# First attention of a four-layer kernel: the multiply by the inverse input scale moves from VectorE to ScalarE

## What is computed

```python
def _div_clamp_fp8(x, scale):
    y = jnp.clip(x.astype(jnp.float32) / scale, -FP8_MAX, FP8_MAX)
    y = y.astype(jnp.bfloat16).astype(jnp.float32)
    return _fp8_roundtrip(y)

def _fp8_linear_pertensor(x, wq, w_scale, in_scale):
    xq = _div_clamp_fp8(x, in_scale)
    return jnp.einsum('bsi,oi->bso', xq * in_scale, wq) * w_scale

ln_out = _ln(hidden_states, ln_w, ln_b)
q = _ln(_fp8_linear_pertensor(ln_out, wq, wq_scale, q_in_scale).reshape(...), qln_w, qln_b)
k = ...; v = ...
core = _gqa(q, k, v)
qx = ...; kx, vx = the context's projections
xout = _gqa(qx, kx, vx)
catq = _div_clamp_fp8(jnp.concatenate([core, xout], axis=-1), proj_smooth)
return jnp.einsum('bsi,oi->bso', catq, wproj) * (proj_in_scale * proj_w_scale)
```

## Time and profile before

| | |
|---|---|
| median of 3 runs | 1549.01 us (1548.94 to 1551.25) |
| the profiled execution | 1549.62 us, span 1547.8 us |
| mean granted TensorE clock | 0.982 |
| busy, share of the span | TensorE matmul 94%, VectorE 59%, ScalarE 48%, GpSimd 34% |
| first attention | from the start to about 474 us |

### The profile page before, as it was taken

How to read it: one execution, slowest core, us unless ns; L and a number is a source line. 1 busy time by engine, 2 the same in 40 slices (tenths; PEclk the granted TensorE clock), 3 DMA queues, 4 the chain that set the end, 5 groups by cost and what they waited for, 6 DMA issues and landing times. The chain is left out here.

```text
span 1547.8 us, 22216 instructions
## 1 busy us (share of the span) xinstructions
PE 1450.4 (94%) x6910; PEld 1040.0 (67%) x6910; DVE 911.0 (59%) x1972; ACT 749.6 (48%) x2052; POOL 527.3 (34%) x519
## 2 busy tenths in 40 slices
PE   3999999899989999999999999999968999989998
PEld 1677777777774565557787979777745666665656
DVE  7899988899975342323465454554677555553322
ACT  3888788888872211110343535343456555544210
POOL 2667577877761000000542424222111333321000
PEclk9999999999999999999999999999979999999999
DMA  4201000200006411112100000002041000001110
GB/s 197 89 32 61 5 5 1 94 1 1 1 1 271 162 54 51 52 50 75 65 1 1 1 1 1 28 0 78 28 194 45 0 1 1 1 28 35 51 63 22
DMA packets 21304, 71.66 MB, mean 46 GB/s; under 512 B 3858, under 2 KB 6290, under 8 KB 18244
## 3 DMA queue, kind: packets, MB, share of 16 engines
q1 hardware_dynamic: 12980, 57.37, 9.9%
q10 hardware_dynamic: 8208, 12.87, 2.6%
HBM read 69.01 MB, written 1.22 MB: 45 GB/s over the span
## 5 line engine op out<-in xcount | busy, mean ns | idle before, releaser
L1170 ACT ACTIVATE l0f_silu<-bank 128x512 f32<-128x512 f32 x48 | 28.6, 597 | 199.4 <-PE bank L1094 183.1
L808 POOL TENSOR_TENSOR l0a_stepped<-l0a_y,l0a_m 128x512 f32<-128x512 bf16 x64 | 74.1, 1158 | 99.6 <-DVE l0a_m L573 99.1
L1273 DVE TENSOR_TENSOR l0f_product<-l0f_silu,bank 128x512 f32<-128x512 f32 x48 | 32.9, 687 | 124.7 <-ACT l0f_silu L1170 124.5
L836 POOL TENSOR_TENSOR l0a_head_rstd<-l0a_head_var,all_minus_half 128x4 f32<-128x4 f32 x96 | 99.2, 1038 | 6.9 <-DVE l0a_head_var L602 6.9
L749 ACT ACTIVATE l0a_work<-bank,l0a_neg_max 128x128 f32<-128x128 f32 x256 | 90.5, 368 | 5.3 <-DVE l0a_neg_max L615 5.1
L1710 DVE TENSOR_TENSOR all_weights_a<-bank,all_cols 128x512 f32<-128x512 f32 x64 | 43.9, 690 | 79.3 <-PE bank L1539 47.3
L1106 PEld LDWEIGHTS bank<-all_weights_a,l0f_hidden 128*128 128x128 f32 x384 | 72.9, 190 | 25.2 <-issue 16.7
L1106 PE MATMUL bank<-all_weights_a,l0f_hidden 128*128 128x256 f32 x384 | 88.9, 379 | 0.0
L425 PEld LDWEIGHTS bank<-l0a_k_t,l0a_q_t 128*128 128x128 f32 x512 | 64.3, 191 | 33.8 <-ACT l0a_q_t L735 27.4
L2588 POOL TENSOR_TENSOR l3a_q_scale<-l3a_q_var,all_minus_half 128x4 f32<-128x4 f32 x32 | 32.4, 1013 | 159.7 <-DVE l3a_q_var L2378 159.7
L2298 PE MATMUL bank<-l3a_f_xn_t,all_weights_b 128*128 128x512 f32 x192 | 86.2, 593 | 0.0
(11 more groups left out here) (434 smaller groups left out, 3801.0 us busy)
## 6 DMA issues: line engine op xcount, KB each, us to landing
l0f_spread<-l0f_weights ACTq DMA_DIRECT2D x32, 192.0 KB, 2.7
all_weights_a<-in_l_w_q SPq DMA_DIRECT2D x2, 2048.0 KB, 14.2
l0f_spread<-l0f_weights ACTq DMA_DIRECT2D x32, 128.0 KB, 2.9
all_weights_b<-in_l_e_gate_up SPq DMA_DIRECT2D x1, 3200.0 KB, 10.2
all_weights_b<-in_l_e_gate SPq DMA_DIRECT2D x1, 3072.0 KB, 10.7
all_weights_a<-in_l_e_up SPq DMA_DIRECT2D x4, 768.0 KB, 6.9
all_weights_a<-in_l_e_down SPq DMA_DIRECT2D x1, 3072.0 KB, 15.4
l3a_spread<-l3f_weights SPq DMA_DIRECT2D x10, 256.0 KB, 3.5
```

The costliest lines, as they stand in the source:

```text
L808: done = g.tensor_tensor(stepped[:, 0:n], value, step, ALU.add)
L836: g.tensor_tensor(head_rstd[:, m % 2, :], head_var[:, m % 2, :], res.minus_half[:, 0:HU], ALU.pow)\
```

## The change

The multiply leaves VectorE. ScalarE does it in two activations (one for each chunk of 128 features, since the scale is one column for each), of 128 x 128 elements each, from `ln_t` to `yq16`. `scale_input` is last in ScalarE's list, due in steps 1, 3 and 7, so behind the squares of those steps; the early parts are scaled in steps 5, 7, 23 and 31 of tile 3. The waits for GpSimd's end with `yq16` (`quant_done`, `early_done`) move along to ScalarE, and VectorE waits for a new semaphore of ScalarE instead. The first tile's part is scaled ahead of ScalarE's first weight work.

```diff
+        quant_scaled = Steady(mem, "l0a_quant_scaled", 3)
+        early_scaled = mem.sem("l0a_early_scaled")
-        EARLY_TILE, EARLY_QUANT = 3, [6, 8, 24, 32]
+        EARLY_TILE, EARLY_SCALE, EARLY_QUANT = 3, [5, 7, 23, 31], [6, 8, 24, 32]
@@ VectorE
-            def quantise_part(b, i):
-                core, t = divmod(b, TILES)
+            def quantise_part(i):
                 part = slice(i * D, (i + 1) * D)
-                v.tensor_tensor(yq16[:, part].rearrange("p (c n) -> p c n", c=KC), ln_t[:, :, t * P:(t + 1) * P],
-                                along(inv_in[:, KC * (core + i):KC * (core + i + 1)], P), ALU.mult)
                 return split(yq16[:, part], mq16[:, part], D)
...
-                v.wait_ge(ln_ready, TILES)
-                quant_done.wait(v, quant_done.at(b - 1, i + 1))
-                if b == TILES + 2 and i > 0:
-                    v.wait_ge(early_done, len(EARLY))
-                quantise_part(b, i).then_inc(quant_split.sem, 3 // quant_parts(b))
+                quant_scaled.wait(v, quant_scaled.at(b, i + 1))
+                quantise_part(i).then_inc(quant_split.sem, 3 // quant_parts(b))
 
             def quantise_early(k):
-                if k > 1:
-                    v.wait_ge(early_done, k - 1)
-                quantise_part(*EARLY[k]).then_inc(early_split, 1)
+                v.wait_ge(early_scaled, k + 1)
+                quantise_part(EARLY[k][1]).then_inc(early_split, 1)
@@ ScalarE
+            def scale_part(b, i):
+                core, t = divmod(b, TILES)
+                for c in range(KC):
+                    at = KC * (core + i) + c
+                    done = act.activation(yq16[:, (KC * i + c) * P:(KC * i + c + 1) * P], ln_t[:, c, t * P:(t + 1) * P],
+                                          ACT.Copy, scale=inv_in[:, at:at + 1])
+                return done
+
+            def scale_input(b, i):
+
+                b += 1
+                if b == VTS or i >= quant_parts(b):
+                    return
+                quant_done.wait(act, quant_done.at(b - 1, i + 1))
+                if b == TILES + 2 and i > 0:
+                    act.wait_ge(early_done, len(EARLY))
+                scale_part(b, i).then_inc(quant_scaled.sem, 3 // quant_parts(b))
+
+            def scale_early(k):
+                if k > 1:
+                    act.wait_ge(early_done, k - 1)
+                scale_part(*EARLY[k]).then_inc(early_scaled, 1)
...
+            scale_input(-1, 0)
             high(0)
...
+                               (scale_input, [1, 3, 7]), in_tile(EARLY_TILE, scale_early, EARLY_SCALE),
```

## The result

The changed kernel takes 1542.6 us (median of 7 runs, 1540.0 to 1545.1) against 1548.8 for the kernel before (7 runs). The ratio is 0.9961 with a 95% interval of 0.9951 to 0.9970: faster by 6.2 us, between 4.6 and 7.6. Forecast was 1543.2, with a range of 1535 to 1548.

What follows compares the result with a forecast made beforehand. VectorE was taken to set the pace, partly standing behind GpSimd's tensor operations. The terms -4.5 - 1.0 - 0.9 + 0.6 gave -5.8 us, so 1543.2 us, with a range of 1535 to 1548.

Steps and rivals of the forecast that it cites:

- What bounds the kernel: First attention: VectorE sets the pace, but its two-SBUF-input and short bf16 operations stand until GpSimd's tensor operation is over.
- Third parts: Nine parts, six tiles' third and the last three early ones: removing the multiply saves 0.5 us each, 4.5 us.
- First and second parts: 19 ordinary parts of both passes from the third tile on: GpSimd's chain leaves 0.05 us saved each, 1.0 us.
- the two behind weight operations: Two multiplies behind a GpSimd subtraction held up by a weight operation: about 0.45 us saved each, 0.9 us.
- ScalarE's work after the first tile: Added scaling, 0.6 us a part, hidden by ScalarE's idle time before squares: cost taken as 0, bounds 0 to 3 us.
- a margin of 1.29: Second pass, step 4: exponentials end 1.29 us before VectorE wants them; 0.9 us of lateness leaves 0.4.
- 1.1 us of TensorE's idle time a tile: Second pass: idle time before turns takes up a query turned 0.6 to 0.9 us late.
- its 0.4 us a tile: Price if the exponentials' cover goes: VectorE waits 0.4 us a tile at worst, at 0.8 us a part.
- Rival C: ScalarE and TensorE become the bound through exponentials and turned query: about 7 us slower, 1556 us; chance 0.08.
- a sign of C: TensorE waiting above 1 us a tile for the turned query, and VectorE waiting for L749, would show ScalarE and TensorE bounding.
- The first tile's 0.6 us: First tile: VectorE waits for ScalarE there, so one part of added scaling is paid, 0.6 us.
- The total: Whole kernel: 5.8 us less, 1543.2 us as the median of the runs; this forecast's chance 0.60.

Runs made afterwards that it cites:

- e7: Kernel before, with GpSimd's add and subtraction of the mixed heads on 4 columns instead of 512 after the first two uses; 1523.1 us, ratio 0.9837.
- e3: Kernel before, with 9 of 32 parts (third parts of tiles 10 to 15, last three early parts) scaled by ScalarE; 1542.8 us, ratio 0.9963.
- e1: Kernel before without VectorE's 32 multiplies and nothing in their place, so the projections' inputs are wrong; 1540.2 us, ratio 0.9942.
- e9: Kernel before, with the 23 other parts scaled by ScalarE and the 9 third and late early parts still multiplied by VectorE; 1547.5 us, ratio 0.9996.
- e5: The changed kernel run again without alteration; 1543.9 us, ratio 0.9968 against the kernel before.
- e6: Changed kernel with scaling ahead of the square and at other steps, a repeat run on the chip of the changed kernel's repeat; 1539.3 us, ratio 0.9942.
- e4: Changed kernel with scaling ahead of the square, first and second parts both in step 1, three early parts in earlier steps; 1541.8 us, ratio 0.9948.
- e2: Kernel before, keeping VectorE's multiply, with ScalarE's 64 activations added at the changed kernel's places into an unread buffer; 1549.6 us, ratio 1.0003.
- e10: The e4 kernel with GpSimd's rstd ahead of the add and subtraction of the mixed heads in its list; 1554.0 us, ratio 1.0043.

## Why the prediction was right, and which step of it failed

**What bounds the kernel: right, with a wider meaning.** VectorE has no wait in a steady tile, and yet part of its time is GpSimd's. e7 shows the standing itself, and that the size of GpSimd's operations is worth 25.5 us, standing and GpSimd's own chain together. The 0.23 us that the prediction gives for a clip was a mask's; a clip that isn't blocked took 0.25 (e7).

**Third parts, 0.5 us each: right.** The timeline after repeats the forecast to 0.02 us in this pair (0.51). Over all nine, e3's trace gives 3.8 us where 4.5 were summed, 0.42 each, net of what ScalarE's nine parts cost there.

**First and second parts, 0.05 each, and 0.9 for the two behind weight operations: near.** e1 has the saving of all parts without ScalarE's price: 7.9 us between first and last `add_to_x` against 6.4 summed; e9's trace shows 2.2 for its parts, where the sum had 1.9. About 1.0 of e1's extra 1.5 us lies in the first half: from the first `add_to_x` to the eighth e1 is 3.8 us shorter, where the terms give some 2.8. Which term takes it isn't settled.

**ScalarE's work after the first tile, at 0: this step failed.** The prediction let it make the exponentials 0.9 us late, against a margin of 1.29, and let 1.1 us of TensorE's idle time a tile take up the rest. It treated lateness as spent at the next wait. The margin did not hold. The waits of the trace after point to lateness that goes round: a late turned query stops TensorE before the scores, the projections behind them on TensorE come later, ScalarE's square waits for these, and the scaling and the exponentials stand behind the square. This round is read from the waits; no run cuts a single link of it. Three tiles on (24.91, 25.28, 25.47) the exponentials were late enough for VectorE to stand 0.3 to 0.5 us at reciprocals, 1.4 us in a tile. The price is shown: 2.4 us (e5 against e6), 2.6 us against e1, and e4's order takes it away with the work unchanged. Part of the tiles' growth may have another cause, since e3's grow too. The prediction's bounds for this term, 0 to 3 us, held it, but its 0.4 us a tile doesn't come out of its own path: with 0.8 us a part, 0.8 - 0.31 + 0.8 = 1.29 is just the margin. Rival C had named the queue place and TensorE's stand, but as a way to a slower kernel. Its sign appeared: in the steady part TensorE waits 8.7 us for the turned query, 1.7 a tile, where the prediction called more than 1 us a sign of C, and VectorE 0.9 a tile for the exponentials. The kernel was faster all the same.

**The first tile's 0.6 us: not confirmed.** The first `add_to_x` came 1.1 us later in the trace after, but 0.9 later in e1's, which has no work added on ScalarE (86.96 against 86.04 us), and 0.6 later in e6's (86.63). In e7's, whose ScalarE and VectorE do the work of the kernel before, it came 2.1 later (88.18). That place moves by such amounts without the term.

**The total: met with luck.** In traces the first attention ended 4.2 us earlier (469.4 against 473.6), not 5.8. In it, by e1's measure, 7.9 us saved against 6.4 summed stand beside 2.6 us of ScalarE's price against 0, and a start 1.1 us later against 0.6. The other 2.7 us of the profiled difference lie behind it, and the forecast had nothing there. That the median came within 0.6 us of the forecast is luck. The stretch behind took 1070.6 to 1076.0 us over the twelve traces, and 1074.9 and 1074.7 for one and the same kernel (e4, e6), and no kernel touched its code. Parts of it move more: from the first `l1a_q_var` to the first `mid_mid_gate_work` it is 313.5 us in the trace after (761.58 to 1075.10) and 316.3 in e5's, the same kernel (761.58 to 1077.90). TensorE's granted clock differs there from trace to trace; from 736 to 790 us it was 0.97 before and 1.00 after:

```profile
736.00:790.00 54.00, 51.90 (x221) 39.53 (x222) 29.76 (x58) 18.95 (x41) 24.09 (x21) 0.97 0.13 47
```

```profile
736.00:790.00 54.00, 52.65 (x243) 40.68 (x243) 30.57 (x59) 19.18 (x44) 24.50 (x21) 1.00 0.07 27
```

That the clock makes the difference isn't shown: e2's trace has 0.97 in this stretch too and takes 1074.5 us behind the first attention, e10's has 1.00 and takes 1075.4. So of the change's 6.2 us, 4 to 5 are explained by the first attention. That the rest is chance is likely, by what one and the same kernel does from trace to trace and by e5 (3.9 us in the medians), but not proved.

## What to carry to other kernels

Before the duration of a removed instruction is taken as its worth, look in the timeline of the other engine whether it ends a fixed time behind something there: then only its unblocked part and its drain can come off, and the next instruction of the kind stands in its stead. Work added to an engine with idle time is free or not by its place in the queue. Here it was nearly free ahead of the instruction that waits and in the step of its longest wait, and cost 2.4 us behind it. Follow lateness round the engines for several tiles, since a margin that holds for one doesn't hold for three.

## What the runs showed of the hardware

- VectorE's instructions with two SBUF inputs, and its short ones on bf16 (uint16), stand while GpSimd's tensor operations on 256 or 512 columns run. In the trace before they end after GpSimd's recorded end by 0.08 us (clip of 128 x 256), 0.15 (128 x 512) and 0.28 (multiply of 128 x 256), as medians. Beside an `rstd` of 4 columns, recorded with 1.0 us, a mask took its 0.23.
- Where both start at the same moment VectorE mostly goes first (11 of 12 in the trace after), and GpSimd's operation takes 1.25 us instead of 1.16. The one that lost (391.29) took 1.23.
- Not expected was how much hangs on the size of GpSimd's operations: 25.5 us of 1548 for 124 of them (e7), the standing and GpSimd's own chain together.
- Two activations of 128 x 128 from SBUF with a scale column took 0.68 us together, four 1.27 (e6).
